# The front of a two-layer kernel: x loaded first and normalised by ScalarE, one bank per down product, the twisted input by block copies

## The reference

```python
xn = _layernorm(x, axis=-1)
# attention branch, its start
h = jax.nn.silu(xn @ down_w + down_b)            # 128 -> 256
XQ, XK, XV = heads(wq), heads(wk), heads(wv)     # of h, and a learning rate from lr_w
# then a scan over 32 steps of 16 tokens, two layer norms, a product with wo and one with up_w

# feed-forward branch
def _twist(x):
    o_r, o_i, p_r, p_i = jnp.split(x, 4, axis=-1)
    return jnp.concatenate([p_r, -p_i, -o_r, o_i], axis=-1)
gf = _global_net(xn.mean(axis=1, keepdims=True), ...)
out = xn
for _ in range(3):
    tf = _coupling_net(out, ...)                  # four small products, gelu between them
    coupling = 0.1 + adaptive_range * (0.7 * gf + 0.3 * tf - 0.5) * 2.0
    out = out + coupling * _twist(out)
```

## Time and profile before

| what | us |
|---|---|
| median of 3 runs | 486.31 (486.05 to 487.7) |
| the profiled execution | 487.49 |
| its span | 485.7 |
| x is there for DVE | 6.60 |
| first projection product on PE | 28.24 |
| first move of the cycles on DVE | 51.44 |
| the scan's block begins on ACT | 111.80 |

### The profile page before, as it was taken

The page is one execution under the profiler, slowest core; times in us unless marked ns, Lnnn a source line. Parts: engine busy times, 40 slices in busy tenths (PEclk is TensorE's granted clock), DMA queues, the critical chain, the costliest instruction groups (busy, mean ns, idle before and its releaser), DMA issues. The chain is left out here.

```text
span 485.7 us, 10292 instructions
## 1 busy us (share of the span) xinstructions
PE 390.9 (80%) x3168; PEld 266.0 (55%) x3168; DVE 307.6 (63%) x1066; ACT 291.9 (60%) x707; POOL 196.3 (40%) x279
## 2 busy tenths in 40 slices
PE   0799999986999999999970999973898456785990
PEld 0443444335777777777750577762543142665890
DVE  4664726333777777777761357777489896365096
ACT  1266858583666677666651446663578925696634
POOL 1001736403588888888863600005415760000003
PEclk9999999998899999999995579995899876997996
DMA  8120223243122222222123510000000001000003
GB/s 232 22 49 28 67 68 98 69 120 119 42 57 62 65 60 64 65 65 65 49 84 90 118 21 1 2 0 1 0 1 1 1 0 23 1 1 1 0 1 86
DMA packets 35355, 23.06 MB, mean 47 GB/s; under 512 B 10478, under 2 KB 35068, under 8 KB 35324
## 3 DMA queue, kind: packets, MB, share of 16 engines
q1 hardware_dynamic: 34908, 22.55, 17.3%
q10 hardware_dynamic: 416, 0.13, 0.1%
HBM read 13.20 MB, written 9.47 MB: 47 GB/s over the span
## 5 line engine op out<-in xcount | busy, mean ns | idle before, releaser
L449 PE MATMUL bank<-w,hT 128*128 128x385 f32 x128 | 45.6, 496 | 0.6 <-ACT stage L577 0.6
L906 ACT ACTIVATE win<-bank 128x384 f32<-128x384 f32 (+1 forms) x124 | 43.1, 399 | 0.0
L835 PE MATMUL bank<-win,wst 128*32 128x128 f32 x1024 | 42.7, 282 | 0.0
L449 PEld LDWEIGHTS bank<-w,hT 128*128 128x128 f32 x128 | 23.2, 189 | 25.0 <-issue 12.7
L1167 ACT ACTIVATE std_<-mv_,cst 128x2 f32<-128x2 f32 (+1 forms) x46 | 13.5, 296 | 37.2 <-DVE mv_ L1147 20.3
L1380 POOL TENSOR_TENSOR win<-win,lng 128x512 f32<-128x512 f32 x2 | 2.5, 1265 | 77.1 <-ACT win L1661 77.1
L835 PEld LDWEIGHTS bank<-win,wst 128*32 128x32 f32 x1024 | 25.3, 110 | 8.0 <-issue 0.6
L1396 PE MATMUL bank<-xn1T,w1e 128*128 128x512 f32 x32 | 17.7, 676 | 12.4 <-ACT he L1557 12.1
L973 POOL TENSOR_SCALAR xh<-raw,bmv,brs 128x128 f32<-128x128 f32 x32 | 25.4, 793 | 3.0 <-DVE brs L1025 2.9
L830 PE MATMUL bank<-win,cst 128*128 128x128 f32 x128 | 25.6, 283 | 0.7 <-DVE grad L1072 0.7
L966 POOL TENSOR_TENSOR xkm<-win,wst 128x256 f32<-128x256 f32 x32 | 19.6, 613 | 15.0 <-PE bank L852 12.7
(11 more groups left out here) (300 smaller groups left out, 1193.6 us busy)
## 6 DMA issues: line engine op xcount, KB each, us to landing
rows_scratch<-stage SPq DMA_DIRECT2D x32, 192.5 KB
win<-rows_scratch SPq DMA_DIRECT2D x32, 192.5 KB, 2.4
attn_scratch<-ob SPq DMA_DIRECT2D x32, 64.0 KB, 1.6
att<-attn_scratch SPq DMA_DIRECT2D x32, 64.0 KB
xt<-in_L_attn_x SPq DMA_DIRECT2D x4, 256.0 KB, 5.9
out<-win SPq DMA_DIRECT2D x4, 256.0 KB, 2.4
cst<-in_constants SPq DMA_DIRECT2D x1, 535.5 KB, 4.3
w<-in_L_attn_wk SPq DMA_DIRECT2D x2, 128.0 KB, 4.9
```

Source lines behind the costliest of these rows:

```text
L449: mm = nc.tensor.matmul(rows_bank(i, h)[:, 0:RC], hT[:, k, i * P:(i + 1) * P], w4[:, k, h, :], start=(k == 0), stop=(k == 1))
L835: mm = nc.tensor.matmul(dst[32 * b:32 * b + 32, 0:F], v[:, at:at + 2 * K], w_sb[:, state, first_slot(b) + h, :], start=False, stop=(h == 1 ...
L906: nc.scalar.activation(w_sb[:, state, at:at + n, :], bank[b][:, 0:n * F].rearrange("f (h g) -> f h g", h=n), ACT.Copy).then_inc(w_done, 1)
```

## The change

- SP issues x before the constants. Of the table only the identity (128 columns) is loaded early, behind the second batch; `down` stands behind the third; the rest of the table comes in the late group.
- ACT issues `lr_w` (two loads), `lr_b`, `cn_w1` and `cn_b1` between its own instructions, and counts them in `proj_in`. A square root of a constant stands ahead of the real ones.
- DVE's statistics are interleaved with the scales and the copies. `xn` is made by ACT as Identity with scale 1/std and bias minus mean/std, which DVE writes to `nshift`.
- PE's transposes and down products are interleaved; a down product has a bank of its own. The first four units of the projection use banks 0 to 3.
- The twisted input is two copies of 64 partitions for a batch on POOL; its signs are multiplied into `alpha` and `beta`.
- `scan_constants` is cut in two; the larger part stands behind `alpha`. `head_constants` stands between the two halves of `second`.

```diff
@@ SP
-                    sp.dma_start(cst[:], const).then_inc(cst_in, 16)
                     for b in range(B):
                         sp.dma_start(xt[:, b * TPB:(b + 1) * TPB, :], ...).then_inc(x_in[b], 16)
+                        if b == 1:
+                            sp.dma_start(cst[:, 0:P], const[:, 0:P]).then_inc(cst_in, 16)
+                        if b == 2:
+                            load(sp, down_in, down[:], a["L0_attn_down_w"])
...
-                        load(sp, proj_in, w4[:, :, h, 3 * F], col(a["L0_attn_lr_w"][h, 0], 2))
-                    load(sp, proj_in, lrb[:], a["L0_attn_lr_b"].partition_broadcast(P))
                     sp.wait_ge(cleared, 2)
+                    load(sp, late_in, cst[:, P:], const[:, P:])
...
@@ DVE
-                    for b in range(B):
-                        s = slice(b * TPB, (b + 1) * TPB)
-                        dve.wait_ge(std_done, b + 1)
-                        ch.link(nc.vector.reciprocal(rstd[:, s], std[:, s]))
-                        for i in range(b * TPB, (b + 1) * TPB):
-                            nc.vector.tensor_scalar(xn[:, i, :], xt[:, i, :], mv[:, i, 0:1], rstd[:, i:i + 1],
-                                                    ALU.subtract, ALU.mult).then_inc(xn_done, 1)
-                        if b:
-                            turned_copy(b - 1)
-                    turned_copy(B - 1)
+                    def scales(b):
+                        s = slice(b * TPB, (b + 1) * TPB)
+                        dve.wait_ge(std_done, b + 1)
+                        ch.link(nc.vector.reciprocal(rstd[:, s], std[:, s]))
+                        ch.mark(nc.vector.scalar_tensor_tensor(out=nshift[:, s], in0=mv[:, s, 0], scalar=-1.0,
+                                                               in1=rstd[:, s], op0=ALU.mult, op1=ALU.mult))
+                        scaled_at.append(ch.n)
...
-                        nc.vector.scalar_tensor_tensor(out=hT[:, m, t * 512:(t + 1) * 512], in0=bank[n % 4][:, :],
+                        nc.vector.scalar_tensor_tensor(out=hT[:, m, t * 512:(t + 1) * 512], in0=bank[n][:, :],
...
-                            dve.wait_ge(twisted, b + 1)
+                            dve.wait_ge(twisted, 2 * (b + 1) + 1)
@@ PE
-                    for n in range(8):
-                        t, m = divmod(n, 2)
-                        pe.wait_ge(v_chain, turned_at[t])
-                        if n >= 4:
-                            pe.wait_ge(hT_done, n - 3)
-                        nc.tensor.matmul(bank[n % 4][:, :], down[:, m * P:(m + 1) * P], xnT[:, t * 512:(t + 1) * 512],
-                                         start=True, stop=True).then_inc(down_mm, 1)
+                    def hidden(t):
+                        pe.wait_ge(v_chain, turned_at[t])
+                        for m in range(2):
+                            nc.tensor.matmul(bank[2 * t + m][:, :], down[:, m * P:(m + 1) * P], xnT[:, t * 512:(t + 1) * 512],
+                                             start=True, stop=True).then_inc(down_mm, 1)
...
-                    for b in range(B):
-                        if b < 2:
-                            pe.wait_ge(stage_done[1], b + 1)
-                            pe.wait_ge(lr_done, 2 * (b + 1))
-                        else:
-                            pe.wait_ge(twisted, b - 1)
-                        nc.tensor.matmul(bank[6 + b % 2][:, :], con("twist"), xnT[:, cols(b)], start=True, stop=True).then_inc(twist_mm, 1)
@@ ACT
+                    def normed(b):
+                        act.wait_ge(v_chain, scaled_at[b])
+                        for i in range(b * TPB, (b + 1) * TPB):
+                            act.activation(xn[:, i, :], xt[:, i, :], ACT.Identity, bias=nshift[:, i:i + 1],
+                                           scale=rstd[:, i:i + 1]).then_inc(xn_done, 1)
+                    load(act, down_in, down_b[:], col(a["L0_attn_down_b"], 2))
+                    act.wait_ge(v_chain, 1)
+                    act.activation(warm[:], eps[:], ACT.Sqrt)
...
-                    for b in range(B):
-                        act.wait_ge(twist_mm, b + 1)
-                        act.activation(tw0[:, cols(b)], bank[6 + b % 2][:, :], ACT.Copy).then_inc(twisted, 1)
@@ POOL
+                    for b in range(B):
+                        pool.wait_ge(v_chain, turned_at[b])
+                        for n, (to, frm) in enumerate(((0, 64), (64, 0))):
+                            pool.wait_ge(twisted, 2 * b + n + 1)
+                            nc.gpsimd.tensor_copy(tw0[to:to + 64, cols(b)], xnT[frm:frm + 64, cols(b)]).then_inc(twisted, 1)
```

More of the change, by code:

```diff
@@ L59, in constants @@
     put("ident", p == q)
-    tw = np.zeros((P, P))
-    for dst, src, sign in ((0, 2, 1), (1, 3, -1), (2, 0, -1), (3, 1, 1)):
-        for i in range(32):
-            tw[32 * src + i, 32 * dst + i] = sign
-    put("twist", tw)
+    put("sign", np.where((p // 32) % 3 == 0, 1.0, -1.0))
     put("tri", same & (p <= q))
@@ L225, in layer0_in @@
         v_chain, cleared = sem("v_chain", c), sem("in_cleared", c)
-        turned_at, small = [], []
+        turned_at, scaled_at, small = [], [], []
         bias_mm, w4_done = sem("bias_mm", c), sem("w4_done", c)
-        loads = {down_in: 0, proj_in: 0, late_in: 0}
+        ON_ACT = 5
+        loads = {down_in: 0, proj_in: 16 * ON_ACT, late_in: 0}
         def load(eng, group, dst, src):
@@ L505, in _ @@
                             rows_of(i, h)
+                    pe.wait_ge(proj_in, loads[proj_in])
+                    for b in range(B):
+                        pe.wait_ge(stage_done[b // 2], b % 2 + 1)
+                        pe.wait_ge(lr_done, 2 * (b % 2) + b // 2 + 1)
+                        first(0, b)
                     pe.wait_ge(late_in, loads[late_in])
                     pe.wait_ge(hT_done, 8)
-                    for b in range(B):
-                        first(0, b)
-                    pe.wait_ge(stage_done[0], 1)
-                    pe.wait_ge(lr_done, 1)
                     for k in range(2):
-                        mm = nc.tensor.matmul(bank[4][0:1, 0:HD], post_b[:, k:k + 1], wo_raw[:, k, :],
+                        mm = nc.tensor.matmul(bank[5][0:1, 0:HD], post_b[:, k:k + 1], wo_raw[:, k, :],
                                               start=(k == 0), stop=(k == 1))
@@ L610, in couple, with also, deviation @@
                                        scale=beta[:, 0:1]).then_inc(coupled, 1)
-                    load(act, down_in, down[:], a["L0_attn_down_w"])
-                    load(act, down_in, down_b[:], col(a["L0_attn_down_b"], 2))
-                    act.wait_ge(cst_in, 16)
-                    for b in range(B):
+                    def also(dst, src):
+                        act.dma_start(dst, src).then_inc(proj_in, 16)
+                    def deviation(b):
                         act.wait_ge(stats_done, b + 1)
                         s = slice(b * TPB, (b + 1) * TPB)
-                        act.activation(std[:, s], mv[:, s, 1], ACT.Sqrt, bias=con("eps5")).then_inc(std_done, 1)
+                        act.activation(std[:, s], mv[:, s, 1], ACT.Sqrt, bias=eps[:]).then_inc(std_done, 1)
+                    def normed(b):
[6 more added lines that the diff above has]
+                    act.activation(warm[:], eps[:], ACT.Sqrt)
+                    for h in range(H):
+                        also(w4[:, :, h, 3 * F], col(a["L0_attn_lr_w"][h, 0], 2))
+                    deviation(0)
+                    also(lrb[:], a["L0_attn_lr_b"].partition_broadcast(P))
+                    deviation(1)
+                    normed(0)
+                    deviation(2)
+                    normed(1)
+                    also(cw1[:], a["L0_ffn_cn_w1"])
+                    also(cb1[:], a["L0_ffn_cn_b1"].rearrange("(p o) -> p o", o=1))
+                    deviation(3)
+                    normed(2)
+                    normed(3)
                     act.wait_ge(down_in, loads[down_in])
-                    act.wait_ge(proj_in, loads[proj_in])
                     for n in range(8):
```

89 lines of the change are left out of this document (56 added, 33 removed).

## The result

The changed kernel takes 475.84 us (median of 4 runs, 474.02 to 475.96) against 486.41 of before on the same chip: ratio 0.9771, interval 0.9745 to 0.9796. The forecast was 477.9. The low end of the range, 475.5, lies inside the spread of the runs; the gain was 10.6 where 8.4 was forecast. The profiled execution is the fastest of the four, 474.02 with a span of 472.2, the same 1.8 apart as before.

A forecast was written before the change was run, and what follows sets the result against it. A front chain of loads, DVE, PE and the hT loop, then PE up to the gelu, was taken to bound the kernel. Savings of 5.0 + 3.4 = 8.4 gave 479.1 profiled, 477.9 as median; range 475.5 to 482.3.

The forecast's parts named there:

- The loads: Start of the front: without constants and down ahead of it, x lands at 3.8 instead of 6.60, bounds 3.6 to 4.8.
- Normalising: Front, DVE statistics, ACT scaled copies and PE transposes by batch: batch 0's down products start at 11.75.
- The down products on a slow TensorE: PE's down products, slow then fast within batch 1: projections start at 23.2 instead of 28.24, 5.0 saved, bounds 22.3 to 24.8.
- Rival C: Front: x at 3.5, short transposes, ACT's copies shorter than profiled; gain 10, time 476.3; chance 10%.
- Banks: End of the front: with a bank each, hT is not the limit, weights' difference done at 22.7, projections at 23.2.
- Projections to gelu: From the projections to the second layer's gelu: twist's 3.78 goes, 3.4 saved, between 3.0 and 3.8.
- The two short waits: Between projections and gelu: waits for ACT's units in banks 0 to 3, costing up to 0.4.
- What could be late next: SP's late loads, POOL's twisted input and scan constants stay hidden: cost nothing, at most 0.5 for the scan constants' copies.
- The statement on contention: POOL's copies can hold DVE's nshift and weights' difference by up to 0.7 each; counted 0, 0.7 kept in the range.
- The sum: Whole kernel: 5.0 + 3.4 = 8.4 saved, the 66 to the scan's start unchanged; 477.9 predicted.

The follow-up runs named there:

- Constants first: Changed kernel with the whole table of constants loaded ahead of x again: 476.89 us, ratio 0.9781 against the kernel before.
- the second execution: Changed kernel run and profiled once more with no edit: 474.76 us, ratio 0.9751 against the kernel before.
- transposes first: Changed kernel with PE making all four batches' transposes ahead of the eight down products again: 479.63 us, ratio 0.9812 against the kernel before.
- four banks: Changed kernel with the eight down products sharing banks 0 to 3 again, first four projections in banks 4 to 7: 476.93 us, ratio 0.9794 against before.
- twist on PE: Changed kernel with the twisted input made by four PE products and four ACT copies again, not by POOL: 480.34 us, ratio 0.9858 against before.
- the second executions of both: The kernel before and the changed kernel, each profiled again without edits: 486.35 us and 474.76 us.
- the version with loads spread: Changed kernel plus five zero products on PE, POOL held behind DVE's four sums, ACT's small loads except down_b later, fourth batch's statistics earlier: 470.74 us, ratio 0.9658.
- small loads later: Changed kernel with ACT issuing down_b and lr_w behind its first square root instead of ahead of it: 474.53 us, ratio 0.9745 against before.

## Why the prediction was right and wrong

**The loads.** Right in kind; x came at 4.52, 0.7 behind the 3.8 taken, within the bounds of 3.6 to 4.8. The runs name the cause, `down_b`'s 1 KB beside x (3.69 or 3.93 without it). Constants first costs 2.1 at the statistics.

**Normalising.** The first products at 11.61 (11.75 forecast), by errors that cancel: x was 0.7 later, the first transposes came 4.54 behind it where I had 4.85 (0.11 of this is the scales, 0.34 for 0.45), ACT's second batch followed 1.64 behind the first where I had 1.95 with a root between, and the products began 0.91 behind the second transposes where I had 1.15. DVE would have done as well.

**The down products on a slow TensorE: this step failed.** I let TensorE get fast in the middle of batch 1's products, between 16.3 and 18.8. It did at 13.3, and at about 15 in the second execution. From 11.61 on the profiled execution shows, beside what I had put: batch 0's products 2.54 (3.45), transposes 0.44 (1.1), batch 1's products 1.72 (2.5), transposes 0.44 (0.9), the rest 3.43 (3.4). These differences are 2.8 of the 3.0 by which the projections came before 23.2; in the second execution they are 1.8 of 2.0, since batch 0's products were slow to their end. My mistake was to count TensorE's work in two ways. The 5.1 that it took in the kernel before run from the transposes at 18.30 to the load at 23.43, so they hold transposes; in the new order I counted from the first product, and called its 4.6 the same. Counted as before, from the first transposes that I had at 8.65, the change would have come at about 13.8 (an estimate), between the two that were measured. TensorE had made transposes from 9.06 on, with 0.55 idle among them, and they count, as the comparison behind "transposes first" shows. Rival C had nearly the right time (476.3) and named the short transposes, but with x at 3.5 and shorter copies of ACT, which were not so.

**Banks.** That `hT` is not the limit with a bank for each product was right: with four banks 1.9 of waiting come back. There was little to spare, though: DVE's difference of the weights ended at 19.91, and the projections began at 20.18.

**Projections to gelu.** 3.8 for 3.4, at the bound I gave; "twist on PE" gives 3.7 of it to the twist. The two short waits that I had set against it did not appear.

**What could be late next.** Nothing was. The statement on contention held where I had left it in the range: `nshift` beside a copy of POOL took 0.57 instead of 0.16 (DVE 13.05 beside POOL's 12.99), the statistics at 10.80 beside the copy of 10.95 stayed at 0.86, and the two `hT` at 17.59 beside the copy of 17.70 at 1.41, as in the earlier trace rows. By the Trainium skill (SBUF — State Buffer, "Who interferes with whom") of these three just the instruction with two SBUF inputs is shut out; the trace agrees in all three. Where I did not use that rule was the cycles: I carried their 66.3 over unchanged, though the earlier trace rows show DVE's sum held by POOL, and this term, 1.0, depends on which of the two begins first.

**The sum.** Forecast 5.0 + 3.4 + 0 = 8.4; at the scan's block 12.9 were measured, 12.1 between the second executions of both. The medians show 10.6 and 12.3; what lies between is in the stretch behind, which took 373.9 and 372.5 in the two profiled executions of before, 373.3 and 372.6 in those of after, and scatters by more over the variants. Undone one at a time, the order of the loads costs 1.8 to 2.8 at the projections, the interleaving 2.8 to 3.8, the banks 1.7 to 2.6 and the normalising nothing, in all 6.3 to 9.2, where all together gave 7.1 to 8.1. The square root's early table load and the new place of `head_constants` have no run of their own. What stays open: why TensorE's change comes 4.2 after its first work in one execution and some 6 after it in another of the same program (3.9 in "constants first"), and whether the transposes at 13.36 and 16.46 of the kernel before, with 0.84 and 0.72 idle behind them, counted for anything.

## What to carry to other kernels

Before you add up products at a slow clock, find in the weight loads where the change falls, and count the work ahead of it, transposes too, in the same way before and after; then give that term a range of its own, since the change moved by some 1.7 between two executions of one program, and the projections behind it by 1.0. Where two engines share two-input work, ask who begins first: holding the one that nobody waits for was worth 2.6 here. And before moving a load behind other work, look for everyone who waits on its semaphore, not only for who reads it.

## What was not expected of the hardware

The granted clock of the profile reads 1.00 over the slow stretch at the start of a program, though the weight loads go at half their pace; once TensorE had been fast and fell back, it reads 0.50, which is 1.2 of 2.4 GHz. Windows of the changed kernel and of the version with loads spread (length, busy times of PE, PEld, DVE, ACT, POOL, clock, DMA share, GB/s):

```profile
12.00:13.40 1.40, 1.40 (x3) 0.44 (x2) 1.33 (x7) 1.29 (x4) 0.63 (x2) 1.00 0.97 94
```
```profile
12.50:14.00 1.50, 1.50 (x3) 0.46 (x2) 0.16 (x1) 1.50 (x5) 0.75 (x2) 0.50 0.46 60
```

Both stretches have three instructions of PE and weight loads of 0.34. With one load of 1 KB, `down_b`, issued beside the first batch of x DVE's first statistics began at 4.40, with none at 3.69 or 3.93. And a DMA issued by ACT takes 0.35 to 0.50 in ACT's program order: four of them held its second root up by 0.9 in "small loads later", while the two at 8.74 and 9.12 in the changed kernel, issued with copies under way, left no gap between these.
